# A fused memory-and-experts kernel: where block 2's normalisation and transposes stand in the first wave

## The reference, cut to what matters

```python
h  = layernorm(x)
k, q, v = h @ Wk + bk, h @ Wq + bq, h @ Wv + bv
alr = 0.1 * sigmoid(h @ Wlr + blr)
# layer 1: h1 = k + silu(k @ W1 + b1); layer 2: pred = h1 + silu(h1 @ W2 + b2)
# grads of sum(mean((pred - v)**2) * alr) by W1, b1, W2, b2; one AdamW step
# retrieved = the same two layers with the new weights, on q
x1 = x + layernorm(retrieved)
z  = layernorm(layernorm(x1)) * g + b
y  = layernorm(x1) + sum over the top 2 of 8 experts of w_e * (gelu(z @ fW1_e + b1_e) @ fW2_e + b2_e)
out = x1 + layernorm(y)
```

## Time and profile before

| | us |
|---|---|
| median of 3 runs (lowest, highest) | 181.81 (181.69, 182.09) |
| profiled execution, its own time | 181.8 |
| span of the profiled execution | 180.0 |
| TensorE busy | 169.6 (94%) |
| VectorE busy | 139.9 (78%) |
| ScalarE busy | 96.2 (53%) |
| GpSimd busy | 26.8 (15%) |
| mean granted TensorE clock | 0.994 |

### The profile page before, as it was taken

One profiled execution on the slowest core, in us unless ns is written; L12 is line 12 of the kernel. 1 busy time (PEld: TensorE's weight loads), 2 busy tenths in 40 slices (PEclk: granted clock), 3 DMA queues, 4 the chain that ended last, 5 costly groups with the idle time before them and its releaser, 6 DMA issues.

```text
span 180.0 us, 3145 instructions
## 1 busy us (share of the span) xinstructions
PE 169.6 (94%) x1044; PEld 137.5 (76%) x1044; DVE 139.9 (78%) x544; ACT 96.2 (53%) x169; POOL 26.8 (15%) x37
## 2 busy tenths in 40 slices
PE   6888999999999999999999999999999999999970
PEld 6534466667746578988989989999999998999960
DVE  2899996988898879897485699676889765448693
ACT  3159776768463793538348346636336725436511
POOL 2460000000003363240000115000016000002011
PEclk9999999999999999999999999999999999999997
DMA  4992000000000000000000000100000100000101
GB/s 108 314 336 72 6 0 4 0 0 2 0 0 4 0 2 0 4 0 0 4 0 2 0 4 0 58 0 4 2 0 0 64 0 0 0 4 2 58 0 58
DMA packets 3567, 4.99 MB, mean 28 GB/s; under 512 B 352, under 2 KB 2016, under 8 KB 3552
## 3 DMA queue, kind: packets, MB, share of 16 engines
q1 hardware_dynamic: 3552, 4.81, 8.6%
HBM read 3.76 MB, written 1.05 MB: 27 GB/s over the span
## 4 chain that ended last, share of the span: by engine, by line
PE 76%; DVE 17%; issue 2%; DMA 1%; ACT 1%; POOL 0%; DVEq 0%; ACTq 0%
PE bank L389 70%; PE bank L397 4%; DVE stats L951 3%; DVE xnT L1235 2%; DVE xnT L1247 2%; DVE mv L954 1%; DVE xn_tok L964 1%; DMA x_tok<-in_x_dram 1%; DVE vpe L959 1%; DVE gate L1182 1%; DVE xnT L1218 1%; PE bank L589 1%; DVE xnT L1101 1%; DVE xn_tok L1132 1%; DVE h_tok L964 1%
## 5 line engine op out<-in xcount | busy, mean ns | idle before, releaser
L1235 DVE SCALAR_TENSOR_TENSOR xnT<-bank,w_tok,xnT 128x128 f32<-128x128 f32 x112 | 31.5, 344 | 21.4 <-PE bank L389 20.9
L343 POOL TENSOR_TENSOR rstd<-vpe,minus_half 128x4 f32<-128x4 f32 (+1 forms) x25 | 23.3, 938 | 149.4 <-DVE vpe L959 135.7
L389 PE MATMUL bank<-z_hi,fW_hi 128*128 128x512 f32 (+1 forms) x67 | 28.7, 430 | 0.5 <-ACT z_hi L740 0.3
L389 PE MATMUL bank<-z_hi,fW_lo 128*128 128x512 f32 (+1 forms) x67 | 25.4, 381 | 0.0
L389 PE MATMUL bank<-z_lo,fW_hi 128*128 128x512 f32 (+1 forms) x67 | 24.9, 384 | 0.0
L389 PEld LDWEIGHTS bank<-fW_sb,sig 128*128 128x128 f32 x192 | 23.1, 192 | 0.8
L389 PE MATMUL bank<-fW_sb,sig 128*128 128x128 f32 x192 | 23.4, 275 | 0.0
L885 ACT ACTIVATE sig<-bank,early_sb 128x512 f32<-128x512 f32 x24 | 15.9, 685 | 10.3 <-PE bank L389 10.3
L389 PEld LDWEIGHTS bank<-fW_sb,h1T 128*128 128x128 f32 x160 | 19.3, 192 | 1.1 <-issue 0.4
L389 PEld LDWEIGHTS bank<-fW_sb,k_tok 128*128 128x128 f32 x160 | 19.5, 192 | 0.8
L885 ACT ACTIVATE k_tok<-bank,early_sb 128x512 f32<-128x512 f32 x20 | 13.5, 687 | 11.6 <-PE bank L389 11.6
(11 more groups left out here) (146 smaller groups left out, 278.4 us busy)
## 6 DMA issues: line engine op xcount, KB each, us to landing
fW_raw<-in_fW_dram SPq DMA_DIRECT2D x1, 1024.0 KB, 8.7
x_tok<-in_x_dram SPq DMA_DIRECT2D x3, 256.0 KB, 5.3
out_dram<-xn_tok SPq DMA_DIRECT2D x3, 256.0 KB, 2.5
early_sb<-in_early_dram SPq DMA_DIRECT2D x1, 268.0 KB, 3.6
late_sb<-in_late_dram SPq DMA_DIRECT2D x1, 264.0 KB, 5.5
x_tok<-in_x_dram SPq DMA_DIRECT2D x2, 128.0 KB, 2.6
b_raw<-in_late_dram SPq DMA_DIRECT2D x16, 4.0 KB
out_dram<-xn_tok SPq DMA_DIRECT2D x2, 128.0 KB, 1.9
```

Of the source, the lines that this page charges most:

```text
L343: pool.tensor_tensor(rstd[:, ln, where], vpe[:, ln, where], minus_half[:, 0:where.stop - where.start], ALU.pow).then_inc(rstd_ready[ln], 1)
L389: return pe.matmul(out_, lhsT, rhs, start=start, stop=stop)
L1235: last = dve.scalar_tensor_tensor(out=y_tok[:, t, :], in0=bank[Y_BANK[m % len(Y_BANK)]][:, i * P:(i + 1) * P], scalar=w_tok[:, t, e:e + 1] ...
```

## The change

It does four things. VectorE issues `x_norm(2)` in wave 0 between `layer1(0)` and `x_norm(3)`, where it stood ahead of the waves. TensorE's and ScalarE's x step of block 2 leaves their prologues and stands in wave 0 behind h1 of block 0. The turns of bank 7 are numbered to match. The `fw` steps have lag 0 in place of 1, the one of ScalarE's prologue is gone, and the last piece stands in the last wave between gw1 of block 3 and q of block 1.

```diff
@@ -206,7 +206,7 @@
         WAVE = ["dh1", "dz2", "z2", "h1", "n2", "z1", "alr", "gw2", "dz1", "v", "gw1", "k", "n1", "kp", "x", "fw"]
 
         LAG = {"dh1": -1, "dz2": -1, "z2": 0, "h1": 0, "n2": 0, "z1": 1, "alr": 0, "gw2": -1, "dz1": -1,
-               "v": 1, "gw1": -1, "k": 0, "n1": 1, "kp": 2, "x": 3, "fw": 1}
+               "v": 1, "gw1": -1, "k": 0, "n1": 1, "kp": 2, "x": 3, "fw": 0}
 
         def wave(w):
 
@@ -219,14 +219,16 @@
                 return
             if w == NB:
                 yield from (("dh1", last), ("dz2", last), ("q", 0), ("dz1", last), ("gw2", last),
-                            ("gw1", last), ("q", 1), ("q", 2), ("q", 3))
+                            ("gw1", last), ("fw", last), ("q", 1), ("q", 2), ("q", 3))
                 return
             for what in WAVE:
                 b = w + LAG[what]
                 if 0 <= b < NB:
                     yield what, b
-
-        TURNS = [("x", 1), ("x", 2)]
+                if (what, w) == ("h1", 0):
+                    yield "x", 2
+
+        TURNS = [("x", 1)]
         FIRST_BANK = (7, 5)
         for w in range(NB + 1):
             TURNS += [step for step in wave(w) if step[0] in ("x", "k", "h1", "dz2", "dz1")]
@@ -501,7 +503,6 @@
             z1_product(0)
             feature_major_x(1)
             k_product(1)
-            feature_major_x(2)
             steps = {
                 "dh1": dh1_product, "z2": z2_product, "v": v_product, "z1": z1_product,
                 "alr": alr_product, "kp": k_product, "q": q_product, "x": feature_major_x,
@@ -805,8 +806,6 @@
             xnT_out(1)
             nsig1_out(0)
             kT_out(1)
-            xnT_out(2)
-            fw1_high(0)
             steps = {
                 "z2": sig2_out, "z1": sig1_out, "alr": alr_out, "kp": kT_out, "q": qT_out, "x": xnT_out,
                 "n1": nsig1_out, "n2": nsig2_out, "fw": fw1_high,
@@ -1064,7 +1063,6 @@
             x_stats(2)
             x_norm(1)
             x_stats(3)
-            x_norm(2)
             dve.wait_ge(early_in, 16)
             for w in range(NB + 1):
                 if w < NB:
@@ -1072,6 +1070,7 @@
                 if w:
                     layer1_back(w - 1)
                 else:
+                    x_norm(2)
                     x_norm(NB - 1)
                 if w < NB:
                     target(w)
```

## The result

The changed kernel takes 182.43 us (median of 8 runs, 182.25 to 182.60) against 181.85 (8 runs, 181.69 to 182.09): the ratio is 1.0032, with a 95% interval of 1.0022 to 1.0042, so it is slower by 0.58 us. 182.35 was forecast. The profiled execution took 182.25 us, with a span of 180.5. The difference is small, 0.3%, but the interval leaves 1 out.

What follows compares the result with a forecast made beforehand. TensorE's unbroken run of matmuls from 14.21 to 45.06 us was taken as the bound. Terms -1.00 (earlier h1), +0.92 (wait) and +0.63 (transposes) sum to +0.55, so 181.8 becomes 182.35 us, range 181.7 to 182.7.

Steps and rivals of the forecast that it cites:

- h1T earlier by 1.00 us: VectorE, block 0: s1 and h1T go ahead of block 2's normalisation, so h1T ends at 13.16 instead of 14.16.
- The wait for bank 7, 0.92 us: TensorE behind h1's transposes: block 2's transposes wait for ScalarE's copy of h1, idle from 14.78 to 15.70.
- The transposes exposed, 0.63 us: TensorE, wave 0: block 2's transposes leave a hole for the full run, adding 0.63 us ahead of z1 of block 1.
- Nothing gives it back: TensorE's matmuls after z1 of block 1 have no hole up to 45.06, so the whole +0.55 us stays.
- The rival *absorbed: Waves 0 and 1: VectorE sets the pace, part of the 0.55 disappears, 181.8 to 182.1 us; chance 0.17.
- VectorE stands where it stood from target(0) on: VectorE behind the two normalisations, 1.02 us each: the sum of its work is unchanged, so no shift from target(0).
- The roundings cost nothing: ScalarE: the prologue's 0.63 us piece goes, the last piece fits a 2.11 us hole before q of block 1; zero cost.
- The rival *faster: TensorE at bank 7: no wait, as h1 is already copied out; sum -0.56 us, time 181.24 us; chance 0.08.
- The clock: Rival: TensorE's new 0.92 us hole lowers the granted clock, giving 183.3 us and up; chance 0.03.
- The step on what else hangs on it: Block 0: alr's consumer on VectorE moves by 0.45 us; dz2's delay stays hidden by 0.37 where it was 0.27.

Runs made afterwards that it cites:

- bank 6 with the memsets late: Changed kernel with block 2's transposes in bank 6 and GpSimd's three memsets held back until VectorE's normalisations end: 181.63 us, 0.9965 of the kernel before.
- the run with the copy first: Changed kernel with ScalarE's copy of h1 of block 0 put ahead of its sigmoid sig2: 182.44 us, 1.0024 of the kernel before.
- the run of the turns alone: Changed kernel with x_norm(2) back in its old place, so only turns and roundings are moved: 183.57 us, 1.0068 of the kernel before.
- the runs with the memsets held back: Changed kernel, block 2's transposes behind z1 of block 1 or in bank 6, GpSimd's memsets held until VectorE's normalisations end: 0.9995 and 0.9965 of the kernel before.
- the run with bank 6: Changed kernel with block 2's transposes in bank 6 instead of bank 7: 181.75 us, 0.9987 of the kernel before.
- The last run: Block 2's transposes in bank 6, block 3's normalisation on GpSimd without waiting for VectorE's of block 2, memsets later: 180.94 us, 0.9924 of the kernel before.
- the first of the two runs: Changed kernel with block 2's transposes in bank 6, block 3's normalisation on GpSimd behind VectorE's of block 2, memsets later: 181.20 us, 0.9963 of the kernel before.
- roundings alone: Kernel before with only ScalarE's W1 roundings moved, the last piece ahead of q of block 1: 182.12 us, 1.0012 of the kernel before.

## Why the prediction was right

All times of the changed kernel are moved here by 0.09 us, so that the zeros agree.

- **h1T earlier by 1.00 us.** Right: it ended at 13.15 (13.16 forecast), and z2 started at 13.21 (13.21). The step called sig1 just in time for s1; here it had 0.27 us in hand (11.31, s1 at 11.58). In one other execution, that of bank 6 with the memsets late, it did hold s1 up by 0.09.
- **The wait for bank 7, 0.92 us.** Right in size and releaser: the idle time in front of L399 is 0.92 in the profile. The transposes start at 15.69 (15.70). The two runs that take the wait away (another bank, or a product between) bring the stage under the kernel before; the run with the copy first splits it into 0.14 and 0.78.
- **The transposes exposed, 0.63 us.** Right: z1 of block 1 has its time from 16.31 on (16.33).
- **Nothing gives it back.** Right: 0.53 at z1 of block 1, 0.54 at the last dh1. The rival *absorbed* falls with the run of the turns alone, where 1.56 us went through whole.
- **VectorE stands where it stood from target(0) on.** Wrong by 0.18: target starts at 15.28, where it started at 15.10. The step took it that the two normalisations would cost 1.02 us each in their new place; the first of them now lies beside GpSimd's memset, and the runs with the memsets held back give the 0.16 back. It stayed hidden, as ScalarE's alr was late as well (VectorE waited 0.26 us for it). dp moved by 0.52 where 0.45 was forecast: alr's sigmoid ended at 18.76, as forecast (18.77), but dp started 0.11 behind it and not 0.03. So dz2 kept 0.28 us of its spare time where 0.37 was forecast. That the step's error did no harm is owed to the wait for alr; in the run with bank 6, where that wait is gone, the same error costs 0.16.
- **The roundings cost nothing.** Right, shown by the run with them alone.
- **The rival *faster*.** Its mechanism, no wait for bank 7, is real, but its price of -0.56 was wrong for a change of this kind alone: it left out that VectorE's dz2 has only 0.27 us to spare. In the run with bank 6 -0.22 was left, and the whole came only with work taken off VectorE as well. (The step on what else hangs on it has the 0.27 and uses it for the delay, not for this rival.)
- **The clock.** Granted 1.00 in the stretch with the hole, and nine tenths or more in all slices but the last, as in the earlier trace rows: no part in it.

The time itself: 182.35 forecast, 182.43 measured, with 0.55 forecast on the stage and 0.54 found.

## What to carry to other kernels

When a step is moved to where its input is ready earlier, look at what it finds in its new place: here two turns of one PSUM bank came to stand back to back, and the copy between them (0.78 us of hole, 0.92 with a sigmoid ahead of it) ate the microsecond that the swap had won. One product between the turns hides all but 0.06 us of it. And count what a hole hid before: transposes that filled idle time were free here, and the same transposes in a full run cost their time, 0.63 us behind a wait and 0.43 without one (14.82 to 15.25 with bank 6). Last, ask which engine is the next bound: with the wait gone it was VectorE, and of TensorE's 0.56 us only 0.22 was left.

## What had not been expected of the hardware

One VectorE normalisation instruction (128x128, one input and the output in SBUF, two per-partition scalars) beside a GpSimd memset took 0.69 us instead of 0.34 and ended 0.09 behind the memset; 0.16 us of it was lost to what follows. The Trainium skill (SBUF — State Buffer, Who interferes with whom) has such instructions and GpSimd's exclude each other for a whole instruction, through a pair of ports that the engines share. The memset of b_raw fits that as to the end: the normalisation ends only when the memset has, though it had started 0.08 ahead of it (12.98 and 13.06). The last run does not fit: VectorE's four normalisations lay beside GpSimd's first two (12.97 to 14.78) and took 1.03 us to the next instruction (13.09 to 14.12), no more than alone. Why the one disturbs and the other doesn't was not tried.

GpSimd's price was a surprise too. Its four normalisations of 128x128 with per-partition scalars took 4.81 and 4.97 us, 1.2 us each on average, where VectorE starts one every 0.255 us. The single ones differ widely: 0.80, 0.95, 1.84 and 1.26 us in the first of the two runs, 0.96, 0.85, 1.35 and 1.84 in the second. The 1.84 fell both times to the one that started at 16.11 us, beside VectorE instructions with both inputs in SBUF (from 16.15 on), and VectorE's dz2 took 0.83 us beside the last one of the first run, where it takes 0.69. So the average is no price of GpSimd working alone, which no run here shows.

The transfers of x did not land at the same time from one execution to the next. VectorE's first statistics started between 3.10 and 3.95 us, and later tiles can be late too: the bank-6 kernel started them at 3.10 but waited 0.28 us more for the next two tiles, and its zero stands at 11.89, where the changed kernel's (3.17) stands at 11.58. That is more than the effect of most of these changes. Counted from a zero behind the landing, the two kernels that should be equal (before, roundings alone) are: 33.39 and 33.40 us.
